# A macaron block with two expert FFNs around attention: FFN blocks of 256 rows with a float32 first layer, one region for the second FFN, attention's projections in float32

## What is computed

```
x = x + 0.5 * ffn(layernorm(x))
x = x + attention(layernorm(x))        # 16 heads of 4, on the left 64 elements
x = x + 0.5 * ffn(layernorm(x))        # the same weights again

def ffn(t):                            # 8 experts, each token goes to its best two
    logits = t @ gate_w.T + gate_b
    top_v, top_i = top_k(logits, 2)
    h = (t @ w0[e].T + b0[e]) * silu(t @ w1[e].T + b1[e])      # 128 -> 256
    y = h @ w2[e].T + b2[e]                                    # 256 -> 128
    return the sum over the two experts of softmax(top_v) * y
```

## Time and profile before

| | us |
|---|---|
| median of 3 runs | 782.08 |
| the profiled execution, its own time | 782.99 |
| its span in the profile | 781.2 |
| first FFN's expert steps | 60.2 to 217.8 |
| attention's batches | 257.6 to 584.4 |
| second FFN's expert steps | 596.7 to 761.8 |

### The profile page before, as it was taken

How to read it: one execution, slowest core, us unless ns; L and a number is a source line. 1 busy time by engine, 2 the same in 40 slices (tenths; PEclk the granted TensorE clock), 3 DMA queues, 4 the chain that set the end, 5 groups by cost and what they waited for, 6 DMA issues and landing times. The chain is left out here.

```text
span 781.2 us, 15382 instructions
## 1 busy us (share of the span) xinstructions
PE 604.0 (77%) x4631; PEld 428.5 (55%) x4664; DVE 487.0 (62%) x1683; ACT 317.8 (41%) x670; POOL 386.1 (49%) x433
## 2 busy tenths in 40 slices
PE   3328999999911568888888888879964999989790
PEld 2226777878700235555555555545443777778670
DVE  5666674433322676888989888898523654434673
ACT  2203333333300026666666666556752333324230
POOL 4876760000057974454767674423324655535361
PEclk9999999999965558999999999999996999989995
DMA  9434434222111111111222121111102322324433
GB/s 296 94 82 110 117 100 110 73 74 74 35 49 49 54 51 51 46 48 47 74 61 65 61 67 46 48 45 39 51 15 62 79 79 71 92 59 119 158 105 134
DMA packets 68102, 60.30 MB, mean 77 GB/s; under 512 B 11256, under 2 KB 60056, under 8 KB 67224
## 3 DMA queue, kind: packets, MB, share of 16 engines
q1 hardware_dynamic: 57496, 40.67, 18.6%
q0 software_dynamic: 8704, 17.97, 7.4%
q10 hardware_dynamic: 1824, 0.69, 0.4%
HBM read 31.09 MB, written 27.84 MB: 75 GB/s over the span
## 5 line engine op out<-in xcount | busy, mean ns | idle before, releaser
L1073 DVE TENSOR_REDUCE attn_nm<-ps 128x2 f32<-128x512 f32 x256 | 169.4, 684 | 47.3 <-PE ps L778 45.3
L885 ACT ACTIVATE attn_pt<-ps 128x512 f32<-128x512 f32 x256 | 147.3, 596 | 72.1 <-PE ps L762 70.2
L778 PE MATMUL ps<-attn_ka,attn_qa 128*128 128x256 bf16 x512 | 107.7, 297 | 56.2 <-DVE attn_nm L1073 28.9
L331 POOL DMA_INDIRECT x_rows<-route_xn,route_rows x128 | 128.2, 1002 | 44.1 <-issue 35.8
L567 DVE TENSOR_TENSOR experts_act<-ps,experts_silu 128x512 f32<-128x512 f32 x80 | 55.3, 691 | 128.1 <-PE ps L514 101.3
L543 ACT ACTIVATE experts_silu<-ps 128x512 f32<-128x512 f32 x80 | 47.9, 599 | 187.5 <-PE ps L506 158.1
L614 POOL DMA_INDIRECT y_tokens<-experts_y_tokens,experts_to x80 | 78.6, 983 | 70.0 <-DVE experts_y_tokens L578 56.0
L762 PE MATMUL ps<-attn_qa,attn_ka 128*128 128x256 bf16 x512 | 100.3, 280 | 4.4 <-ACT attn_pt L885 2.4
L524 PE MATMUL ps<-w_table,experts_actT 128*128 x640 | 95.6, 286 | 1.9 <-DVE experts_y_tokens L578 1.8
L778 PEld LDWEIGHTS ps<-attn_ka,attn_qa 128*128 128x128 bf16 x512 | 40.4, 102 | 90.9 <-DVE attn_nm L1073 52.1
L524 PEld LDWEIGHTS ps<-w_table,experts_actT 128*128 128x128 f32 x640 | 85.8, 195 | 3.9 <-issue 2.8
(11 more groups left out here) (168 smaller groups left out, 1024.6 us busy)
## 6 DMA issues: line engine op xcount, KB each, us to landing
experts_x<-x_rows SPq DMA_DIRECT2D x160, 65.0 KB
y_rows<-experts_y_tokens SPq DMA_DIRECT2D x40, 128.0 KB, 1.8
second_y<-y_tokens SPq DMA_DIRECT2D x16, 256.0 KB, 4.2
kq_pieces<-attn_kqp SPq DMA_DIRECT2D x16, 192.0 KB
x_rows<-no_rows SPq DMA_DIRECT2D x32, 65.0 KB
x_rows<-route_xn,route_rows POOLq DMA_INDIRECT x128
out<-x_tokens SPq DMA_DIRECT2D x16, 128.0 KB, 1.8
x_tokens<-x SPq DMA_DIRECT2D x7, 256.0 KB, 8.8
```

The costliest lines, as they stand in the source:

```text
L331: nc.gpsimd.indirect_dma_start(out=x_rows[group_turn(g)[0] % 2][:, :], out_offset=to, in_=xn[:, g % RX, t, :], in_offset=None).then_inc(se ...
L778: mm = pe.matmul(ps[:, SA[k], j * S:(j + 1) * S], qa[sl][:, h, qc * P:(qc + 1) * P], ka[sl][:, h, :], start=True, stop=True)
L885: nc.scalar.activation(pt[:, g % 2, j, :], ps[:, SBK[h % 2], :], ACT.Exp, scale=SCALE).then_inc(exp_done, 1)
L1073: nc.vector.tensor_reduce(nm[:, qc, 2 * pair:2 * pair + 2], ps[:, SA[k], :].rearrange("p (j t) -> p j t", t=S), AX.X, ALU.max, negate=True ...
```

## The change

- **Blocks of 256 rows, one expert each.** `SLOTS` goes from 128 to 256. Worst-case counts: 19 + 27 = 46 steps in the first FFN, 17 + 22 = 39 in the second, which now has one region for all 8 groups, in parts of 6 and 2 groups. A part that leaves the region open lists only blocks that are sure to be full, and has no tails.
- **First layer in plain float32, weights stationary.** Each step copies its expert's weights (128x512 float32) from the table in SBUF to one of 6 buffers by a DMA on SP's queue (`w`), and makes four float32 products of 256 columns whose result has the hidden units on the partitions. So the turning of the activations, the splits and the bias product are gone; the bias comes in as a per-partition column of silu and of the multiplication (`pe_cols`, `act_cols`). ACT copies x and y; VectorE does not.
- **The token's weight** travels with the row (`XCOLS` 130 to 132) and is applied when y is copied (`act_y`), so that the end only adds.
- **Attention's projections** in float32 on 64 rows, without splits.
- **The end**: all 16 batches are read back behind the last scatter, half by SP and half by ACT.
- **SP's order in the first FFN**: at the second part the four first loads are issued together, late.
- `POOL`'s rstd and DVE's statistics run three groups ahead instead of two.

```diff
-TURN_GROUPS = (3, 5, 5, 3)
-SLOTS = 128
-PAIRS = tuple(-(-((2 * n * T + E * (SLOTS - 1)) // SLOTS) // 2) for n in TURN_GROUPS)
+PART_GROUPS = (3, 5, 6, 2)
+REGION_OF = (0, 1, 2, 2)
+SLOTS = 256
+def part_blocks(part):
+    whole = [i for i in range(part + 1) if REGION_OF[i] == REGION_OF[part]]
+    rows, ragged = 2 * T * sum(PART_GROUPS[i] for i in whole), E * (SLOTS - 1)
+    earlier = sum(part_blocks(i) for i in whole[:-1])
+    return ((rows + ragged) // SLOTS if closed(part) else -(-(rows - ragged) // SLOTS)) - earlier
...
     def pe_first(pe, q):
-        for i in range(2):
-            e, o = expert[2 * q + i], ps[:, q % 2 * 2 + i, :]
-            hi, lo = m["x_hi"][:, q % 2, i], m["x_lo"][:, q % 2, i]
-            pe.matmul(o, hi, streamed(w_table, e, W1H, 2 * HID), start=True, stop=False)
-            pe.matmul(o, hi, streamed(w_table, e, W1L, 2 * HID), start=False, stop=False)
-            pe.matmul(o, lo, streamed(w_table, e, W1H, 2 * HID), start=False, stop=False)
-            mm = pe.matmul(o, streamed(chosen, e, 0, P), b_table[:, 0:2 * HID], start=False, stop=True)
+        pe.wait_ge(w_in[q % WR], 16 * (q // WR + 1))
+        for k in range(CH):
+            wait(pe, act_done, CH * (q - 2) + k + 1)
+            for w, at in enumerate((W1, W0)):
+                mm = pe.matmul(ps[:, q % 2 * 2 + k, w * SLOTS:(w + 1) * SLOTS], m["w"][:, q % WR, at + k * P:at + (k + 1) * P],
+                               m["xT"][:, q % 2], start=True, stop=True)
...
-    def pe_turn(pe, q):
-    def dve_xlo(dve, q):
-    def dve_y(dve, q):
+    def act_y(act, q):
+        wait_out(act, q - YR)
+            for i in range(2):
+                a = nc.scalar.activation(m["y_tokens"][:, q % YR, i], ps[:, Y, i * P:(i + 1) * P], ACT.Copy,
+                                         scale=m["weight"][:, q % IR, i:i + 1])
...
     def sp_list(sp, part):
+        if closed(part):
             for at in route["tails_of"](sp, part):
...
     def sp_x(sp, q):
         wait(sp, xT_ready, q - XR + 1)
         wait(sp, to_ready, q - XR - ONE + 1)
+        sp.dma_start(m["x"][:, q % XR], rows_of(x_rows[REGION_OF[part] % 2], start[q])).then_inc(x_in[q % XR], 16)
+        wait(sp, h_ready, CH * (q - WR + 1))
+        sp.dma_start(m["w"][:, q % WR], of_expert(w_table, owner[q], 0, WCOLS)).then_inc(w_in[q % WR], 16)
...
     def sp(sp, q, own):
+        if q - Y_LAG - 1 in own and q - Y_LAG - 1 < ONE:
+            sp_y(sp, q - Y_LAG - 1)
+        starts = [own.start] + [first_block(part) for part in range(1, SECOND) if first_block(part) in own]
+        late = [range(n, n + XR) for n in starts]
+        for ns in late:
+            if q == max(ns.start - AHEAD - 1, own.start - AHEAD):
+                for n in ns:
+                    sp_x(sp, n)
+        n = q + AHEAD + XR - 1
+        if n in own and not any(n in ns for ns in late):
+            sp_x(sp, n)
...
     def pe_project(pe, b):
-        pe.matmul(ps[:, MISC_A, 0:S], wqk_hi[:], xT[:], start=True, stop=False, skip_group_check=True)
-        pe.matmul(ps[:, MISC_A, 0:S], wqk_lo[:], xT[:], start=False, stop=True, skip_group_check=True)
+        pe.matmul(ps[:, MISC_A, 0:S], wqk[:], xT[:], start=True, stop=True)
...
-                if q == middle + HALF_OUT:
-                    blocks["out_to"](sp, middle)
-                    sp_load(sp, range(EARLIER))
             blocks["out_to"](sp, own.stop)
-            sp_load(sp, range(EARLIER, NB))
+            for b in range(0, NB, 2):
+                load(sp, b)
+            for b in range(0, NB, 2):
+                store(sp, b)
```

More of the change, by code:

```diff
@@ L180, in bank, with closed_parts, listing @@
         return BANK[g]
+    def closed_parts(part):
+        return len([i for i in range(part) if closed(i)])
+    def listing(part):
+        return sum(8 + 3 * carried(i) + 3 * (not closed(i)) for i in range(part))
     def tile(g, t):
@@ L570, in dve_xlo @@
[L570 to L579 removed]
+        part, at = block_part(q)
@@ new lines, in dve_act @@
+        wait(dve, y_ready, q - 1)
+        if at == 0:
+            dve.wait_ge(route["cols_done"], part + 1)
+        for k in range(CH):
+            dve.wait_ge(silu_done, CH * q + k + 1)
+            nc.vector.scalar_tensor_tensor(out=m["act"][:, q % 2, k], in0=ps[:, q % 2 * 2 + k, SLOTS:2 * SLOTS],
+                                           scalar=route["col"](part, at, CH + k), in1=m["silu"][:, q % 2, k],
+                                           op0=ALU.add, op1=ALU.mult).then_inc(act_done, 1)
@@ L597, in dve @@
+        dve.wait_ge(to_step, 3 * n + 3)
+        nc.vector.scalar_tensor_tensor(out=m["to"][:, q % IR], in0=const["dumped"], scalar=float(n * SLOTS),
+                                       in1=m["row"][:, q % 2], op0=ALU.add, op1=ALU.min)
+        nc.vector.tensor_tensor(m["weight"][:, q % IR], m["more"][:, q % 2], weights[:, :, 0], ALU.add).then_inc(to_ready, 1)
     def dve(dve, q, own, between):
@@ L1649, in _ @@
                     route["act_tanh"](act, LAST)
+                if q == begin + TOP + 5:
+                    route["act_cols"](act, PARTS - 1)
+            blocks["out_to"](act, own.stop)
+            for b in range(1, NB, 2):
+                load(act, b)
+            for b in range(1, NB, 2):
+                store(act, b)
         @block.gpsimd
```

723 lines of the change are left out of this document (366 added, 357 removed).

## The result

The changed kernel takes **753.47 us** (median of 4 runs, 752.53 to 754.61) where the kernel before took 782.84 in the same runs: a ratio of 0.9626, 95% interval 0.9606 to 0.9647. The forecast was 758, with a range of 743 to 781. The time fell by 29.4 us instead of 24.

The account below looks back on a forecast made before the run. TensorE was taken to bound both FFNs, waits to bound attention. First FFN +0.7, second -32.1, DMA +2, attention -5.5 and end +11.0 gave -23.9 from 783.0, so 759.1; forecast median 758 us, range 743 to 781.

Parts of the forecast that it names:

- the allowance for DMA: Both FFNs: the weight copies fit, but rows land later when sends go beside them; +2 us (0 to 10).
- the signs that I had named: Right if: FFN steps of 3.0, stall of 5 to 8 at step 19, then clock 0.5, 28 to 32 us behind last product.
- The step: One step of either FFN: four products at 0.44, transposes 0.22, second layer 1.03; 3.01 us (2.13 to 3.27).
- The stalls: TensorE waiting for a new part's first rows: first FFN 7.0 plus 3.2 slow clock, second FFN 4.8 plus 3.2 us.
- their landing 2.93: First FFN's second part: time for the tails to land before the first rows, 2.93 us of an 11.8 us sequence.
- The second FFN: 39 steps 117.4, drain 0.8, start 3.8, turn's stall 4.8 plus 3.2, GpSimd 3: 133.0 against 165.1, so -32.1 us.
- 8.8 are left for the start and the routes, which I keep: First FFN: of 12.8 us beyond the steps, 4.0 is drain; the other 8.8 stays unchanged.
- GpSimd's +3 in the second FFN: Scatters take 2.54 of each 3.01 us step, so the last group's eight sends are only partly absorbed; +3 us (0 to 8).
- the chain gains only what lay on it, 0.5 to 0.6 at eight of the batches: Attention: chain of keys and queries through DRAM shortens, -4.5 us, plus 1 at the last batch's end; -5.5 in all.
- at 293 GB/s: The end: 6.3 MB of loads and results take 21.5 us at this rate, 23 with the start; end 30.4, +11.0 us.
- The end of 24.2: Behind the last product, by the skill's 2.0 us plus bytes at 436 GB/s: loads 11.6, whole time 752 us; chance 0.05.
- The row buffers: Rival: row buffers become the second FFN's loop; at a landing of 5 us, step 3.7, whole time 785 us; chance 0.08.

Follow-up runs that it names:

- a_now: The changed kernel without the copies of the weights behind the first six of each FFN; 747.91 us, 5.4 under the changed kernel.
- b_pad: The kernel before with one pair of transposes of attention's prologue repeated eight times (16 more); 847.59 us against 846.42 for the kernel before, ratio 1.002.

## Why the prediction held, point by point

**The sum: right, in part by luck.** Five stretches came out better than forecast, by 16.6 us together: the start (2.9), the gap (0.4), the way to the second FFN (6.0), the end (5.3) and the allowance for DMA (2.0). Three came out worse, by 10.0: the first FFN (5.6), attention (4.1) and the second FFN (0.3). The difference, 6.6, is how far the forecast fall of 23.9 missed the 30.4 of the profile. Of the signs that I had named, the steps of 3.0, the stall at step 19 and its clock of 0.5 came. The last product is 36 us earlier, not 30, and 25 us lie behind it, not 28 to 32. One sign of being wrong nearly came too: attention's span hardly changed.

**The step.** 0.44 per product was forecast, 0.445 measured, 3.01 for the step against 3.06. The way to 0.44 was weaker than its result. The prediction read the second layer as four float32 products in 1.03 us, 0.26 each, and then took 0.22 "without its start-up", which no row shows. The second layer of the kernel before also holds two bf16 products, which add the bias. In the step of the earlier trace rows:

```profile
650.55 0.22 PE L525 MATMUL ps<-b_table,chosen 128*128 128x128 bf16 x1
650.61 0.66 PE L524 MATMUL ps<-w_table,experts_actT 128*128 x4
```

Two float32 products, each in two of the rows that the profile counts, fill 650.10 to 650.55, so one of 128 columns takes 0.22, and 256 columns take twice that.

**The stalls.** In the first FFN 7.0 of standing still and 3.2 of slow clock were forecast, 7.8 and 2.5 measured; at the second part 4.8 and 3.2 against 6.3 and 1.6. Both sums are right (10.2 against 10.4, 8.0 against 7.9), because errors cancel, and that is luck. The term that failed is "their landing 2.93": from the last tail to the first rows pass 4.8 and 5.6 us. The prediction had nothing for SP's second load of registers, 2.06 and 2.27 us, which stands there. Not the size of the tails made it long: a_now writes tails as large, without that load, and has 2.7 and 3.0. In the first FFN the tails' issue (4.0 instead of 4.8) and the first rows' landing (2.1 instead of 2.7) gave most of it back.

**The second FFN, -31.8 against -32.1.** The steps give 25.5 of it, from 144.8 to 119.3. The stall behind the early loads gives 5.8 with its slow clock (first products of before at 722.96, 731.89 and 735.96, 13.00 for two steps of 3.62). The part's own stall costs 7.9 where it cost 6.7.

**First FFN, +6.3 instead of +0.7.** The term "8.8 are left for the start and the routes, which I keep" and the step are what failed. 46 x 0.05 are 2.3. The routing of the last groups lies between short steps now: eleven steps from the first are 41.5 us, 7.9 beyond 3.06 each, against 46.2 and 6.4 beyond 3.62 each: 1.5. The step at 161 lost 1.0. There TensorE's own load of the experts' registers runs until 162.86, and the transposes, due at 162.2, start at 163.03:

```profile
L502 PEldq TENSOR_LOAD <-route_listed x1: 3519/3519/3519, 159.3 to 159.3; - x1
```

In a_now this load takes 2.40, and the step loses nothing. Why it is shorter there is open. The rest, about 1, is the drain. Against the wide forecast each is small, but all have one sign.

**GpSimd's +3 in the second FFN.** It did not come as a stall of its own. Beyond steps and stall the second FFN has 133.2 - 119.3 - 7.9 = 6.0, of which 2.6 lie in its first two steps, which route the last group, and about 2 in the drain. The forecast had 3.8 + 0.8 + 3 for these.

**Attention, -1.4 instead of -5.5.** The step that failed is "the chain gains only what lay on it, 0.5 to 0.6 at eight of the batches". What was removed lay on VectorE at positions 5 to 7 of a batch. The chain runs from position 3 through DRAM. In it nothing became shorter: from a batch's start to the write of the pieces are 6.74 us before (456.15 to 462.89) and after (461.70 to 468.44). SP's rows of the changed kernel, the write among them:

```profile
466.28 1.19 SPq L1268 DMA_DIRECT2D attn_qa<-attn_mT  x2
468.44 0.39 SPq L1242 DMA_DIRECT2D kq_pieces<-attn_kqp  x1
```

A second term was missing. The prediction priced what left VectorE and GpSimd, and nothing for the projections on TensorE, which now has 4.0 us more to do in eight batches.

**What no term had.** The stretch behind attention, -6.0, of which 5.6 are the barrier's wait, and the earlier start, -2.9. The prelude was costed at nothing, as covered by GpSimd's sends. But the kernel also changed how far GpSimd's and VectorE's preparation runs ahead, and the first transposes came at 56.84 instead of 60.27. Which part of the prelude gave it was not tried apart.

**The end, +5.7 instead of +11.0.** Two steps failed. Loads start 4.9 us behind the last product, not 7.4. And "at 293 GB/s" was the rate of another mix of transfers, at a DMA share of 0.93: at the end the engines moved 364 GB/s when full. The Trainium skill, "DMA: Bandwidth & Descriptors", section "Anatomy of one DMA — SWDGE (gpsimd) path", gives 436 GB/s behind a fixed 2.0 us, for a DMA that GpSimd issues; these are issued by SP and ACT. The end of 24.2 that I worked out from it is nearer to 25.2 than my 30.4, but it holds the same start of 7.4, and the terms shown there add to 23.0 to 23.8. With the measured start of 4.9 and all 6.3 MB at the page's rate the end would be 21.3, an estimate, and with mine 27.9. Here the runs sit between the two: 364 measured with loads and stores mixed.

**The DMA allowance, +2.** No run shows a cost of the copies. A steady step is 3.06 with them and without, and the two stalls that a_now shortens are shorter by SP's load of registers.

So of the 30.4 us between the two spans, 31.8 came from the second FFN, 6.0 and 2.9 from two places that I hadn't looked at and 1.8 from attention and the gap before it; 6.3 were given back in the first FFN and 5.7 at the end. The rivals did not come. The row buffers never held a steady step (3.06), and the DMA share stayed near 0.5.

## What to carry to other kernels

When steps become shorter, every fixed event between them (a list, tails, first rows of a new part) shows in full. Look in the issuing queue for what can be written earlier: here sixteen tails and four first loads moved by some steps gave 16 us, more than half of the change's own gain. Before a wait is called a landing, see what the waiting engine itself does in it: here a new load of ten registers, 2.1 to 2.3 us, stood between the tails and the rows, and no DMA was under way for 3.3 us of it. Moving that load ahead of the tails was not tried. An edit that leaves out a transfer also leaves out what prepares it, so compare the instructions, too, before the gain is given to the transfer. Removing work from an engine pays only if the work lies on the loop that ends the wait; follow the loop through every queue before pricing it, SP's order too, and price what the edit adds on the other engines.

## What was not expected of the hardware

- At a barrier all engines waited 6.9 us for TensorE's sequencer with one form of attention's code (7.4 in b_pad), and 0.3 to 1.6 with the other, the work being nearly the same.
- A load of ten registers from SBUF took SP 2.1 to 2.9 us at the two stalls, and one took TensorE's sequencer 3.5 us at 159.3.
- The kernel before took 782 to 783 us in the result's runs and on one chip, and 836.6 and 846.4 on two others. There VectorE and ScalarE show 75 to 114 us of gaps that no semaphore explains, and none of the changed kernel's relatives gained more than 1.1% in the median.
- Copies within SBUF of 262 KB in each 3.06 us cost a steady step nothing, at a DMA share of 0.51 to 0.52 and 162 to 167 GB/s.
- With all DMA engines full at the end, 364 GB/s, a quarter above the highest rate in the rows of before (293).
